# A new opening for a fused attention kernel: constant matmuls first, and another order of the query and first key products

## What is computed

```python
q = (layernorm(x) @ Wq + bq) * scale           # 256 x 512
k = ctx @ Wk + bk                              # 4096 x 512
q = fake_quantize(q, per head); k = fake_quantize(k, per head)
```

## Time and profile before

| what | value |
|---|---|
| median of 3 runs | 582.42 us |
| span of the profiled execution | 582.8 us |
| TensorE busy | 531.9 us |
| VectorE busy | 457.6 us |
| ScalarE busy | 364.7 us |
| GpSimd busy | 28.4 us |

### The profile page before, as it was taken

The page is one execution under the profiler, slowest core; times in us unless marked ns, Lnnn a source line. Parts: engine busy times, 40 slices in busy tenths (PEclk is TensorE's granted clock), DMA queues, the critical chain, the costliest instruction groups (busy, mean ns, idle before and its releaser), DMA issues. The chain is left out here.

```text
span 582.8 us, 10649 instructions
## 1 busy us (share of the span) xinstructions
PE 531.9 (91%) x4283; PEld 333.8 (57%) x4286; DVE 457.6 (79%) x858; ACT 364.7 (63%) x431; POOL 28.4 (5%) x28
## 2 busy tenths in 40 slices
PE   3999999999899999999998788699999899996995
PEld 2444555543566656665665565488884565652582
DVE  2599999966899989998999797401593889878995
ACT  5624656464799889988998788400343753586342
POOL 0300000000300200030005100000000000000000
PEclk9999999999999999999998788899999999997999
DMA  8723300042345435553556459603938204300000
GB/s 319 264 74 87 130 1 1 0 142 85 119 148 182 165 107 176 166 168 112 160 177 241 170 165 432 265 1 95 319 163 341 106 0 180 111 0 0 2 2 36
DMA packets 20145, 78.84 MB, mean 135 GB/s; under 512 B 2176, under 2 KB 3200, under 8 KB 16896
## 3 DMA queue, kind: packets, MB, share of 16 engines
q1 hardware_dynamic: 20096, 78.16, 37.8%
HBM read 75.27 MB, written 0.79 MB: 131 GB/s over the span
## 5 line engine op out<-in xcount | busy, mean ns | idle before, releaser
L1122 DVE CUSTOM_DVE_ANT_0 arena<-ps,arena 128x1024 f32<-128x1024 f32 x128 | 152.5, 1220 | 16.2 <-issue 7.7
L1530 ACT ACTIVATE arena<-arena,small 128x4096 int16<-128x4096 f32 x32 | 121.5, 3798 | 2.5 <-DVE small L1135 2.4
L600 PE MATMUL ps<-arena 128*128 128x512 f16 x384 | 100.1, 380 | 0.0
L641 PE MATMUL ps<-small,arena 128*128 128x128 bf16 x1024 | 81.7, 225 | 8.1 <-DVE arena L1142 4.8
L566 PE MATMUL ps<-arena 128*128 128x512 f16 x384 | 85.2, 379 | 1.2 <-DVE arena L1053 1.2
L641 PEld LDWEIGHTS ps<-small,arena 128*128 128x128 bf16 x1024 | 61.1, 100 | 17.8 <-issue 6.9
L1537 ACT ACTIVATE arena<-ps 128x512 int32<-128x512 int32 x96 | 56.9, 593 | 21.7 <-PE ps L641 21.3
L815 PE MATMUL ps<-arena 128*128 128x256 f32 (+1 forms) x288 | 67.3, 397 | 0.7 <-ACT arena L1619 0.7
L815 PEld LDWEIGHTS ps<-arena 128*128 128x128 f32 x288 | 55.7, 194 | 11.8 <-issue 3.3
L566 PEld LDWEIGHTS ps<-arena 128*128 128x128 f16 x384 | 37.2, 98 | 43.6 <-issue 1.5
L657 PEld LDWEIGHTS ps<-arena 128*128 128x128 f16 x1024 | 43.0, 97 | 30.1 <-issue 8.2
(11 more groups left out here) (172 smaller groups left out, 729.5 us busy)
## 6 DMA issues: line engine op xcount, KB each, us to landing
arena<-key_scales SPq DMA_DIRECT2D x64, 512.0 KB, 5.0
arena<-in_ctxT SPq DMA_DIRECT2D x8, 1024.0 KB, 6.8
arena<-in_wg SPq DMA_DIRECT2D x4, 1024.0 KB, 7.2
arena<-in_wo SPq DMA_DIRECT2D x2, 2048.0 KB, 11.6
arena<-in_wu SPq DMA_DIRECT2D x4, 1024.0 KB, 6.9
arena<-in_wd SPq DMA_DIRECT2D x4, 1024.0 KB, 5.8
arena<-in_wuq SPq DMA_DIRECT2D x1, 3072.0 KB, 24.9
arena<-in_wkr SPq DMA_DIRECT2D x1, 2048.0 KB, 13.9
```

What stands on the lines that cost most here:

```text
L600: last = pe.matmul(ps[:, bank, :], wv16[wpart][:, k, g * P:(g + 1) * P], ctx16[cpart][:, k, tok], start=(k == 0 and i == 0), stop=(k == KC ...
L641: last = pe.transpose(ps[:, bank, :].bitcast(BF16)[:, b * P:(b + 1) * P], p16[u % 2][:, (8 * q + b) * P:(8 * q + b + 1) * P].bitcast(BF16) ...
L1122: dve.tensor_tensor_reduce(sc[:, u % 2, i * SCW:(i + 1) * SCW], ps[:, 2 * (n % 2):2 * (n % 2) + 2, :].rearrange("p a b -> p (a b)"), skb[: ...
L1530: act.activation(p16[u % 2], sc[:, u % 2, :], ACT.Exp, bias=ebias[:, u % 2:u % 2 + 1], scale=sq[:, i:i + 1], accum_out=rsum[:, u:u + 1]).t ...
```

## The change

A small constant tile is set by GpSimd, and TensorE multiplies it by itself 16 times into bank 0 before it does anything else. ScalarE stores the turned latents ahead of the bound of extent 1. TensorE does half of the first query tile between the first two maxima, and waits for one stored latent tile rather than both. In key step 0 the products of high parts come first, for all four chunks, then (behind a wait for the first low part and the third maximum) high x low, then low x high. The number of matmuls of the step stays 48.

```diff
+        spin = small([TOK], BF16)
+        spin_set = sem("spin_set")
+            def keep_clock(n):
+
+                pe.wait_ge(spin_set, 1)
+                for _ in range(n):
+                    pe.matmul(ps[:, 0, :], spin[:, 0:P], spin[:, :], start=True, stop=True)
+
-            def project_queries(t):
+            def project_queries(t, ks):
                 pe.wait_ge(ld_wq, 16)
-                pe.wait_ge(s_xnTe, QT)
-                for k in range(KC):
+                pe.wait_ge(s_xnTe, t + 1)
+                for k in ks:
                     last = pe.matmul(ps[:, 4 + t, :], xnT[:, k, t * P:(t + 1) * P], wq_sb[:, k, :],
                                      start=(k == 0), stop=(k == KC - 1))
-                last.then_inc(s_q, 1)
+                if ks[-1] == KC - 1:
+                    last.then_inc(s_q, 1)
+            def project_first_keys(cp):
+
+                chunks = (2 * cp, 2 * cp + 1)
+                parts = [(c, k, 0, 0) for c in range(4) for k in range(KC)] if cp == 0 else []
+                parts += [(c, k, 0, 1) for c in chunks for k in range(KC)]
+                parts += [(c, k, 1, 0) for c in chunks for k in range(KC)]
+                if cp == 0:
+                    pe.wait_ge(xhi, ctx_extent(0) + 1)
+                for n, (c, k, cpart, wpart) in enumerate(parts):
+                    if wpart and c == 0 and k == 0:
+                        pe.wait_ge(xlo, 1)
+                        spread_max(2)
+                    elif cpart and c == 0 and k == 0:
+                        pe.wait_ge(xlo, ctx_extent(0) + 1)
+                    last = pe.matmul(ps[:, c, :], ctx16[cpart][:, k, c * P:(c + 1) * P], wk16[wpart][:, k, :],
+                                     start=(k == 0 and not cpart and not wpart), stop=(k == KC - 1 and cpart == 1))
+                last.then_inc(kproj, 1)
...
+            keep_clock(16)
             pe.wait_ge(ld_id, 16)
             turn_latents()
             spread_max(0)
+            project_queries(0, [0, 1])
             spread_max(1)
-            project_queries(0)
-            project_queries(1)
-            spread_max(2)
+            project_queries(0, [2, 3])
+            project_queries(1, [0, 1, 2, 3])
             for j in range(STEPS):
-                pe.wait_ge(xlo, ctx_extent(j) + 1)
-                project_keys(j, 0)
+                if j:
+                    pe.wait_ge(xlo, ctx_extent(j) + 1)
+                    project_keys(j, 0)
+                else:
+                    project_first_keys(0)
...
+            pool.memset(spin[:, :], 1.0).then_inc(spin_set, 1)
             bias_queries()
...
             bound(0)
+            store_latents()
             bound(1)
-            store_latents()
             high_part(0)
```

More of the change, by code:

```diff
@@ L674, in _ @@
                     turn_queries(j - 3)
-                project_keys(j, 1)
+                if j:
+                    project_keys(j, 1)
+                else:
+                    project_first_keys(1)
                 spread_max(j + 3)
```

## The result

The changed kernel takes 586.54 us (median of 4 runs, 585.04 to 587.52), the kernel before 582.59 (4 runs, 581.97 to 583.61). The ratio is 1.006, with a 95% interval of 1.0033 to 1.0087: slower by 3.5 us by the ratio (3.95 between the medians), somewhere between 1.9 and 5.1. The forecast was 585.6 in a range of 583.4 to 587.4.

The account below looks back on a forecast made before the run. The path was taken to run from query projection through the third maximum, its split and VectorE's key work to TensorE's key step 2. Third maximum +3.45, low part -0.25 gave +3.2 on 582.42: 585.6 us, range 583.4 to 587.4.

Parts of the forecast that it names:

- The place of the third maximum: TensorE, key step 0: 16 high-part products now stand ahead of `spread_max(2)`, delaying it 3.45 us, from 22.96 to 26.4.
- The path behind it: From `spread_max(2)` through the split and VectorE's key work to TensorE's key step 2: first evacuation at 32.0, step 2 at 48.9.
- The sum: Opening: third maximum +3.45 us, low part -0.25, so the first evacuation comes 3.2 us later.
- The second maximum: TensorE, behind half of the first query tile: `spread_max(1)` at 16.3 instead of 12.26, at no cost.
- The low part: VectorE, low part of extent 2: 2.35 us instead of 2.60, as GpSimd's query scaling is over; 0.25 us back.
- The clock: TensorE, opening: falls to 1.2 GHz in the stop before the query projection and rises again about 18.7, as before.
- the first half alone: Rival: TensorE's clock stays at 2.4 GHz through the opening, nothing is gained, 582.6 us; chance 0.08.
- The stops: TensorE waits about 2 us before the second half of key step 1 and 2 us again before key step 2.
- rival two: TensorE around 40 and 47: the new stops bring the clock down, up to 1.7 us more, 587.3 us; chance 0.12.
- the span and the device time are 0.3 us apart: Whole kernel before: profiled span 582.8 against run median 582.42, taken as 0.3 us apart.
- The prediction read the two as running together: VectorE's low part of extent 2 and GpSimd's query scaling: both run at once, the low part 0.25 us longer.

Follow-up runs that it names:

- e4: The kernel before with only key step 0 in the new order, the third maximum behind the 16 products of high parts: 586.55 us, ratio 1.0055.
- e1: The changed kernel with the third maximum moved back directly behind the queries, ahead of the high parts' products: 583.22 us, ratio 1.0003.
- e5: The kernel before in its old order, with 16 constant matmuls at the start and 12 behind the first maximum: 580.57 us, ratio 0.9955.
- e8: The kernel before with only the latents' stores moved and the first query tile split around the second maximum: 582.69 us, ratio 0.9996.
- e3: The changed kernel with 12 more constant matmuls behind the first maximum: 583.61 us, ratio 1.002.
- r1_changed_again: The changed kernel, unaltered, measured a second time: 586.33 us, ratio 1.0051 to the kernel before.
- e2_no_constant: The changed kernel without its 16 constant matmuls, first measurement: 584.66 us, ratio 1.0047 to the kernel before.
- r2_no_constant_again: The changed kernel without its 16 constant matmuls, measured a second time: 586.32 us, ratio 1.0057 to the kernel before.

## Why the prediction was right

**The place of the third maximum** was the whole forecast, 3.45 us. Measured in e4: 25.95 - 22.50 = 3.45. Right.

**The path behind it.** The forecast had the first evacuation at 32.0 and a shift that stays the same from there to key step 2. It came at 31.69, and the shift was 2.93 at all four points. The sum said 3.2. The 0.3 us are the start: the loads came sooner in this execution (the latents by 0.26 us; the query weights, for which the projection waits, let it start at 12.56 for 12.85), and the third maximum moved with them (26.14 for 26.4). The second maximum came at 16.13, forecast at 16.3. The low part took 2.35 us, without GpSimd beside it, as forecast. In e1 and e5 to e8, where GpSimd's work on the queries lies beside the low part again, it took 2.60 or 2.61.

**The clock.** The fall between 9.7 and 12.6 and the rise at 18.5 (18.7 forecast) were right. The Trainium skill, TensorE: Matmul & The Clock Gate, Part 1, names both halves, release by activity and the return when idle; the trace shows both, 1.00 at 11 and 0.50 at 13, and e3 shows what the first half alone is worth: 582.6 was forecast and 583.61 measured.

**The stops.** The first was forecast at about 2 us and was 2.33, at 41.16. The second, ahead of key step 2, should also have been 2 us; the wait list of the changed kernel from 24 to 60 has one more, of only 0.17:

```profile
PE ps L593 <- DVE arena L1087: 2.5, 2, 2.3
```

The time between went into the clock. It was down again, as rival two had it, from 42.4 to 45.8:

```profile
42.00:43.00 1.00, 1.00 (x5) 0.41 (x4) 1.00 (x6) 0.13 (x1) 0.00 (x0) 0.70 0.00 0
43.00:44.00 1.00, 1.00 (x4) 0.39 (x3) 0.97 (x2) 1.00 (x1) 0.00 (x0) 0.50 0.00 0
```

The 24 matmuls took 6.87 us instead of 5.18, 1.7 us more, and the time TensorE had in hand covered them with 0.17 us to spare. In r1_changed_again the clock stayed up in this stretch, and two stops of 0.30 and 1.29 us stood in its place. Rival two's mechanism is thus real; that the fall costs nothing holds by a small margin. The forecast had left the fall out, so that its time stood all the same is in part luck.

**Sizes.** The median rose by 3.95 us, the trace by 2.93. Both lie in the interval of 1.9 to 5.1, and the second set of runs, r1_changed_again, has a ratio of 1.0051, or 3.0 us. Where the other 1 us of the first set comes from is not shown.

The traces do show that a total holds more than the opening. The last column of the table goes from 534.9 to 537.2 us, though nothing behind key step 2 was changed. The executions differ there in when the clock is low: from 310 to 390 us it was granted at 0.85 before, 0.87 after and 0.89 in e1_third_max_first, and from 570 to 580 at 1.00 before and 0.83 in e4_first_keys_alone. So the equal growth of opening and span after the change, 2.9 and 2.9, says less than it seems. What is shown is the 2.93 us at key step 2 of the trace, and the ratios: 1.0047 to 1.006 in the five sets with the third maximum behind the 16 products and the clock not held, 1.0003 and 0.9996 in e1 and e8, where it follows the queries. Whether the place of the later falls follows from the edits was not tested.

Two smaller parts of the prediction did not come out: that the span and the device time are 0.3 us apart (1.8), and that TensorE stands 2 us ahead of key step 2 (0.17, with the clock down in its place).

## What to carry to other kernels

When a short instruction on one engine releases a chain on three others, moving bulk work ahead of it costs that work's full length, even if the total of work is unchanged and the bulk work could run at once. Constant matmuls have to reach up to the real work: sixteen that stop 6 us before the queries bought nothing that the times show, and with twelve more in the gap the path was 2.8 us shorter. And look at the edits one by one: here the ideas that were worth something (the clock held, which takes the twelve further matmuls, and the queries sooner) gave 0.9944 once they were parted from the one that cost 3.45 us. And compare starts in the opening as well as totals, which here moved by 2 us for reasons far behind the edit.

## What the runs showed of the hardware that was not expected

The clock rose anywhere from 15.5 to 18.5 us in kernels whose query instructions all start between 12.50 and 12.77, even for one and the same kernel (15.5 and 18.5 without the constant). In e2_no_constant and r2_no_constant_again that moved key step 2 by 1.6 us. Why it rises at one place or the other was not tested. Single runs of one kernel differ by up to 4 us (r1_changed_again: 583.2 to 587.17), of which the rise can be only a part, since the kernel before differs as much (580.79 to 585.18). A waiting time of 2.33 us, with dense 512-column matmuls on both sides of it, went with a fall to the lower level in four profiled executions (changed, e4, e2, r2_no_constant_again) and without one in two (r1_changed_again, e3).

GpSimd's scaling of the queries took 2.96 us before, when it began 0.54 us behind VectorE's low part, and in the changed kernel, with no such instruction beside it:

```profile
26.49 1.05 POOL L1476 TENSOR_SCALAR arena<-arena 128x1024 f32<-128x1024 f32 x1
```

It thus took 1.9 us more beside the low part, of which it stood beside 2.06. The prediction read the two as running together; these durations are much nearer to what the Trainium skill, SBUF — State Buffer, SBUF: two separate sides, says of the shared port pair, that the one that starts first holds it for its whole instruction and the other waits. GpSimd's 1.05 us counted from the end of the low part (28.84) make 29.89, and it ended at 29.74. The low part's own 0.25 us has a candidate too, in the kernel before:

```profile
24.33 2.36 POOL L1440 TENSOR_TENSOR arena<-arena 128x1024 f32<-128x1024 f32 x1 [23.89 <-ACT arena L1474]
```

The addition of the bias ran 0.45 us into the low part, and it did so by 0.45 or 0.46 us in each of e1 and e5 to e8, where the low part took 2.60 or 2.61. A full wait would have cost 0.45 and not 0.25, so this stays open. None of it changed the sum, for the queries are not needed before `round_queries`.
